# The prologue of a two-stage attention and feed-forward kernel, its TensorE steps in another order

## What is computed

```
q, k, v = relu(x @ Wqkv.T)                      per head of 8 channels
vk      = [v, 1].T @ k                          summed over the 512 tokens
num     = vk @ q ;  att = num[:8] / (num[8] + 1e-15)
x1      = layernorm(x + att @ Wproj.T + bias)
h       = silu(x1 @ Wg.T / 127) * (x1 @ Wu.T / 127)
out     = layernorm(x1 + h @ (Wd / 127).T)
```

## Time and profile before

| | |
|---|---|
| three runs | 490.69, 491.10, 489.64 us (median 490.69) |
| span of the profiled execution | 489.6 us |
| PE busy | 482.2 us, 98% |
| DVE, ACT, POOL busy | 415.5, 255.9, 85.2 us |
| granted TensorE clock, mean | 0.999 |
| first gate product of batch 0 starts | 40.2 us |

### The profile page before, as it was taken

One profiled execution on the slowest core, in us unless ns is written; L12 is line 12 of the kernel. 1 busy time (PEld: TensorE's weight loads), 2 busy tenths in 40 slices (PEclk: granted clock), 3 DMA queues, 4 the chain that ended last, 5 costly groups with the idle time before them and its releaser, 6 DMA issues.

```text
span 489.6 us, 11236 instructions
## 1 busy us (share of the span) xinstructions
PE 482.2 (98%) x4291; PEld 405.5 (83%) x4291; DVE 415.5 (85%) x939; ACT 255.9 (52%) x442; POOL 85.2 (17%) x94
## 2 busy tenths in 40 slices
PE   8999999999999999999999999999999999999996
PEld 5888888878888888888888888888888888879885
DVE  5878878879899797988979889797988979799896
ACT  4667435464455545545555455545555554355553
POOL 1330110402103030210402103030220402113012
PEclk9999999999999999999999999999999999999999
DMA  8425075274754737467283754737467281561212
GB/s 302 179 81 173 11 247 174 89 259 167 252 178 181 251 108 260 142 238 233 89 304 118 253 178 166 263 110 261 143 235 234 87 299 46 175 216 46 86 44 88
DMA packets 67656, 85.29 MB, mean 174 GB/s; under 512 B 4016, under 2 KB 47024, under 8 KB 67632
## 3 DMA queue, kind: packets, MB, share of 16 engines
q1 hardware_dynamic: 67344, 84.70, 50.2%
q10 hardware_dynamic: 288, 0.26, 0.2%
HBM read 48.24 MB, written 36.18 MB: 172 GB/s over the span
## 4 chain that ended last, share of the span: by engine, by line
PE 78%; DVE 11%; DMA 5%; issue 2%; ACT 2%; POOL 1%; SPq 0%; POOLq 0%; DVEq 0%
PE up_ps L1058 28%; PE abcd_ps L1058 22%; PE gate_ps L1058 22%; PE abcd_ps L1110 3%; DVE h L616 2%; PE gate_ps L1088 2%; DMA wd_raw<-x_way 2%; DVE st L685 2%; DVE h_lo L609 2%; DMA x_way<-wu_raw 1%; ACT h_hi L409 1%; DVE r L702 1%; DMA wkv_raw<-att_way 1%; DVE r L737 1%; DMA wqp_raw<-w_q 1%
## 5 line engine op out<-in xcount | busy, mean ns | idle before, releaser
L409 ACT ACTIVATE h_hi<-h 128x512 fp32r<-128x512 f32 (+1 forms) x97 | 60.6, 626 | 72.2 <-DVE h L616 71.7
L331 POOL TENSOR_TENSOR rstd<-ve,minus_half 128x4 f32<-128x4 f32 (+2 forms) x36 | 35.5, 985 | 339.8 <-DVE ve L697 338.6
L609 DVE TENSOR_TENSOR h_lo<-h,h_hi 128x512 fp32r<-128x512 f32 (+1 forms) x97 | 63.3, 678 | 25.6 <-ACT h_hi L409 25.3
L414 ACT ACTIVATE silu<-gate_ps 128x512 f32<-128x512 f32 x95 | 55.9, 588 | 45.6 <-PE gate_ps L1058 45.6
L616 DVE SCALAR_TENSOR_TENSOR h<-up_ps,silu 128x512 f32<-128x512 f32 x95 | 65.1, 686 | 16.6 <-PE up_ps L1058 13.9
L1058 PE MATMUL gate_ps<-x1T_hi,wg_hi 128*128 128x512 f32 x192 | 75.0, 391 | 1.3 <-ACT silu L414 0.7
L1058 PE MATMUL gate_ps<-x1T_lo,wg_hi 128*128 128x512 f32 x192 | 74.8, 390 | 0.0
L1058 PE MATMUL up_ps<-x1T_hi,wu_hi 128*128 128x512 f32 x192 | 74.8, 389 | 0.0
L1058 PE MATMUL up_ps<-x1T_lo,wu_hi 128*128 128x512 f32 x192 | 74.7, 389 | 0.0
L406 ACT ACTIVATE kv<-abcd_ps 128x512 f32<-128x512 f32 x55 | 32.9, 601 | 44.9 <-PE abcd_ps L1058 43.5
L354 POOL TENSOR_TENSOR xb<-x_raw,bias_sb 128x1024 f32<-128x1024 f32 x16 | 38.7, 2420 | 50.0 <-DVE den L639 47.8
(11 more groups left out here) (191 smaller groups left out, 1017.1 us busy)
## 6 DMA issues: line engine op xcount, KB each, us to landing
x_raw<-x_tok SPq DMA_DIRECT2D x16, 512.0 KB, 3.6
att_way<-wg_raw SPq DMA_DIRECT2D x30, 256.0 KB, 3.5
wkv_raw<-att_way SPq DMA_DIRECT2D x30, 256.0 KB, 3.0
xT_raw<-x_chan SPq DMA_DIRECT2D x14, 512.0 KB, 4.4
x_way<-wu_raw SPq DMA_DIRECT2D x28, 256.0 KB, 2.4
wd_raw<-x_way SPq DMA_DIRECT2D x28, 256.0 KB, 3.0
out<-out_sb SPq DMA_DIRECT2D x14, 512.0 KB, 3.4
x_keep<-r SPq DMA_DIRECT2D x12, 512.0 KB, 2.6
```

Of the source, the lines that this page charges most:

```text
L331: nc.gpsimd.tensor_tensor(rs[:, tiles], ve[:, tiles], minus_half[:, tiles], ALU.pow).then_inc(rs_ok, 1)
L409: nc.scalar.activation(dst, src, ACT.Copy).then_inc(ok, 1)
L414: nc.scalar.activation(silu[:, j % 2, :], gate_ps[bank_of(j)][:], ACT.Silu, scale=WSCALE).then_inc(silu_ok[j], 1)
L609: return nc.vector.tensor_tensor(lo, raw, f32(hi), ALU.subtract)
```

## The change

The order of the lists of TensorE, ScalarE and VectorE in the prologue is rewritten, and with it which banks some steps use:

- q of batch 1 moves from before vk of batch 0 to behind vk of batch 1. All four kv tiles of batch 1 now stand before the numerator of batch 0, and vk of batch 1 straight behind it. The banks of the kv tiles of batch 1 change places.
- One tile more of batch 2 stands before the projection of batch 0.
- The turn of x1 of batch 0 and the flag's product move from before the numerator of batch 1 to behind vk of batch 2; the flag's product uses a bank of its own (`flag_ps` in `up_ps1`).
- ScalarE takes relus and sums of squares in an order that fits. VectorE makes xT_lo of batch 2 before the denominator of batch 0, masks vk of batch 1 before attT_lo, and makes x1T_lo of batch 0 behind the denominator of batch 1.

```diff
-        kv1_ps = (gate_ps[0][:], up_ps[0][:], gate_ps[1][:], up_ps[1][:])
+        kv1_ps = (gate_ps[1][:], up_ps[1][:], gate_ps[0][:], up_ps[0][:])
+        flag_ps = up_ps[1][0:1, 0:3]
...
             xT_hi_of(2)
-            q_relu(1, (gate_ps[1][:], up_ps[1][:]))
...
-            kv_relu(0, 1, kv1_ps[0])
+            act.wait_ge(vk_mm, 1)
+            for t in range(NT):
+                kv_relu(t, 1, kv1_ps[t])
             squares_of(0, wg_lo)
-            for t in range(1, NT):
-                kv_relu(t, 1, kv1_ps[t])
+            squares_of(1, wu_lo)
+            q_relu(1, (gate_ps[1][:], up_ps[1][:]))
             attT_hi_of(0)
-            kv_relu(0, 2, kv2_ps[0])
-            squares_of(1, wu_lo)
+            for t in range(2):
+                kv_relu(t, 2, kv2_ps[t])
             squares_of(2, wd_lo)
-            for t in range(1, NT):
+            for t in range(2, NT):
                 kv_relu(t, 2, kv2_ps[t])
...
+            xT_lo_of(2)
             rden_of(0)
             att_of(0, turned=True)
-            xT_lo_of(2)
+            vk_of(1, vk1_ps)
             attT_lo_of(0)
-            vk_of(1, vk1_ps)
...
-            dve.wait_ge(flag_mm, 1)
-            nc.vector.reduce_sum(lo_flag[:], B[0:1, 0:3], AX.X).then_inc(flag_ok, 1)
-            x1T_lo_of(0)
...
             vk_of(2, vk2_ps)
+            dve.wait_ge(flag_mm, 1)
+            nc.vector.reduce_sum(lo_flag[:], flag_ps, AX.X).then_inc(flag_ok, 1)
             rden_of(1)
+            x1T_lo_of(0)
             att_of(1)
...
             pe.wait_ge(xT1_lo_ok, 1)
-            q_of(1, (gate_ps[1][:], up_ps[1][:]), xT1_hi, xT1_lo)
+            kv_of(0, 1, kv1_ps[0], xT1_hi, xT1_lo)
             pe.wait_ge(ones_ok, 1)
             vk_of(0, A)
-            kv_of(0, 1, kv1_ps[0], xT1_hi, xT1_lo)
+            for t in range(1, NT):
+                kv_of(t, 1, kv1_ps[t], xT1_hi, xT1_lo)
             num_inputs(0)
             num_of(0, qT_first)
-            kv_of(1, 1, kv1_ps[1], xT1_hi, xT1_lo)
-            for t in range(2, NT):
-                pe.wait_ge(q_ok[t - 2], 2)
-                kv_of(t, 1, kv1_ps[t], xT1_hi, xT1_lo)
+            vk_of(1, vk1_ps)
+            q_of(1, (gate_ps[1][:], up_ps[1][:]), xT1_hi, xT1_lo)
             pe.wait_ge(consts_in, 16)
             attT_of(0)
-            vk_of(1, vk1_ps)
             pe.wait_ge(xT_lo_ok, 2)
             kv_of(0, 2, kv2_ps[0])
+            pe.wait_ge(q_ok[0], 2)
+            kv_of(1, 2, kv2_ps[1])
             pe.wait_ge(wp_lo_ok, 1)
             proj_of(0)
-            for t in range(1, NT):
+            pe.wait_ge(q_ok[1], 2)
+            for t in range(2, NT):
                 kv_of(t, 2, kv2_ps[t])
-                if t == 2:
-                    pe.wait_ge(squares_ok, 3)
-                    mm(B[0:1, 0:3], ones_col[:], lo_squares[:], start=True, stop=True).then_inc(flag_mm, 1)
-            pe.wait_ge(vk_ok, 2)
-            pe.wait_ge(kv_ok[0], 3)
+            num_inputs(1)
+            for n in range(2):
+                pe.wait_ge(r1_ok[n], 1)
+            pe.wait_ge(kv_ok[NT - 1], 3)
+            num_of(1)
+            vk_of(2, vk2_ps)
+            pe.wait_ge(squares_ok, 3)
+            mm(flag_ps, ones_col[:], lo_squares[:], start=True, stop=True).then_inc(flag_mm, 1)
             x1T_pair(0, r2, x1T_ps, 1)
             x1T_pair(1, r2, x1T_ps, 1)
             pe.wait_ge(flag_ok, 1)
             pe.reg_load(flag, lo_flag[:].bitcast(INT32))
-            pe.wait_ge(kv_ok[NT - 1], 3)
-            num_inputs(1)
-            num_of(1)
-            vk_of(2, vk2_ps)
             q_of(2, q2_ps, ahead_of_second=lambda: pe.wait_ge(vk_ok, 3))
```

## The result

The changed kernel takes **491.84 us** (median of 12 runs, 490.97 to 492.76), the kernel before, in the same comparison, 490.87 us (12 runs, 489.64 to 491.83). The ratio is 1.0019 (95% interval 1.001 to 1.0028), so the change costs about 0.97 us, between 0.5 and 1.4. That is within 0.3%: no difference by the measure that the prediction used, on its slower side.

The account below looks back on a forecast made before the run. TensorE, busy 482.2 of 489.6 us, was taken to bound the kernel. Waits of 0.39, 0.89 and 0.20 us less 0.6 of passages made 0.86, added to the 490.69 median: 491.55 us, range 490.2 to 492.6.

Parts of the forecast that it names:

- Wait 1: Before the turn of batch 0's attention, TensorE stands 0.39 us until VectorE has made att; bounds 0.2 and 0.6.
- Wait 2: Before the numerator of batch 1, TensorE waits 0.89 us for ScalarE's relu to empty bank A; between 0.8 and 1.0.
- Wait 3: Before q of batch 2, TensorE waits 0.20 us for the flag's sum and register load; bounds 0 and 0.55.
- The passages: In the prologue, fewer changes from narrow to wide products on TensorE save about 0.6 us, at about 0.23 us each.
- the third block: Numerator of batch 1, vk of batch 2, flag, then x1's turn and q: passage between 0 and 0.23 us, taken as 0.11.
- The waits are covered: Rival for the prologue: passages save 0.7 us and only half of wait 2 remains, giving 490.4 us; chance 0.09.
- the change doesn't do what it says: Rival: the new order is not really built; given nothing, as the built order shows every step moved.
- The stall near 99 us goes: Rival in batch 2's turn: TensorE's 0.7 us wait for x1T_lo vanishes, giving 490.85 us; chance 0.13.
- The trip of batch 1's att: Slower rival: its second half lands late and the projection waits some 0.75 us, giving 492.3 us; chance 0.08.
- The load was not long: Judges the slower rival at the flag: a register load of 1.3 us gives 492.35 us; chance 0.04.
- VectorE's x1T_lo for gate: Ahead of the first gate product: ready for both halves near 40.2, 0.8 us ahead of gate.

Follow-up runs that it names:

- cover_num: Changed kernel with the first half of q of batch 2 and the flag's product put before the numerator of batch 1: 491.67 us, ratio to before 1.0015.
- load_later: Changed kernel with the flag's register load moved behind q of batch 2: 491.53 us, ratio to before 1.001.
- cover_both: As cover_num, with one tile of batch 2 moved ahead of the turn of batch 0's attention and a third ahead of the projection: 491.31 us, ratio 1.0002.
- tail_only: Kernel before with only the new order from the numerator of batch 1 on, the head as before: 491.74 us, ratio to before 1.001.
- cover_both_again: The cover_both kernel, unchanged, for a second execution under the profile: 491.03 us, ratio to before 1.0000.
- head_only: Changed kernel with the tail of before, flag's product and both turns of x1 ahead of the numerator of batch 1: 491.91 us, ratio to before 1.0024.

## Why the prediction was right

**The forecast.** 491.55 us was foretold and 491.84 measured, with the difference from before +0.86 against +0.97 (and 0.6 the second time). The first gate product was to stand at 41.08 and stands at 40.96. The places foretold on the way held to a tenth: vk of batch 0 at 14.97 (14.97), the numerator at 19.95 (20.01), the turn at 25.03 (25.01), the numerator of batch 1 at 35.20 (35.22), the transposes at 37.18 (37.09). That a sum is right does not show that its terms are; they are taken one by one.

**Wait 1** was put at 0.39 us. q's last product starts at 24.48 (the second of the row at 24.25), the next could start at 24.70, and the turn starts at 25.01: 0.31. The chain from the numerator over den, rden and att to the turn runs as copied from the earlier trace rows. VectorE's rows of after show that step by step:

```profile
21.31 0.29 DVE L641 TENSOR_SCALAR den<-abcd_ps 128x128 f32<-128x128 f32 x1 [0.65 <-PE abcd_ps L1112]
21.64 0.95 DVE L645 RECIPROCAL rden<-den 128x128 f32<-128x128 f32 x1
```

Such a wait need not be in the list of waits: here only the chain and the timeline show it.

**Wait 2** was put at 0.89 us. The last product starts at 34.06, the numerator could follow at 34.38 and starts at 35.22: 0.84, of which the trace marks 0.78 as waiting for kv. It was the dearest term, and it was the bank conflict in the code. cover_num keeps that conflict and puts work over it, and gives 0.60 us of the stretch back net.

**Wait 3** was put at 0.20 us. Against the transposes' own step it looks like 0.11 (their last start is 37.91, the next could be at 38.02, q starts at 38.13). But load_later, where q does not wait, takes it up 0.13 behind the last pair, and the changed kernel 0.33: the wait is 0.20, and its price in the stretch 0.17. What was off is the flag's product. I gave it 0.12 us of its own behind vk, as it takes in the chain of before (at 32.95). In the trace it starts at 36.94, ahead of the last product of vk, and the transposes follow at 37.09 and not at 37.18:

```profile
36.38 0.75 PE L1090 MATMUL gate_ps<-kv 128*32 128x36 f32 x63
36.94 0.17 PE L1323 MATMUL up_ps<-lo_squares,ones_col 128*1 128x3 f32 x1
36.95 0.20 PE L1090 MATMUL gate_ps<-kv 128*32 128x36 f32 x1
```

This did not bring VectorE's sum forward, which starts at 37.42 (37.39 foretold):

```profile
37.42 0.14 DVE L927 TENSOR_REDUCE lo_flag<-up_ps 1x1 f32<-1x3 f32 x1
```

But the load stood closer behind the sum than the 0.29 us that I had read from the earlier trace rows, whose start of the load is rounded to a tenth. It began at 37.6 and not at 37.68, and q 0.12 us before its time. The load's own time was right:

```profile
L1327 PEldq TENSOR_LOAD <-lo_flag x1: 484/484/484, 37.6 to 37.6; - x1
```

The rule of the Trainium skill that was weighed (DMA: Bandwidth & Descriptors, Latency and other measured facts: a floor of about 600 ns for a tensor_load) is not borne out: the load took 0.484 to 0.488 us in the traces shown here.

**The passages** were to save 0.6 us. The waits measured are 0.31 + 0.84 + 0.20 = 1.35, the loss is 0.74, so 0.61 were saved. What was too high is waits 1 and 2, by 0.08 and 0.05, and that makes up the difference of the forecast's 0.86 from 0.74. That the saving came out so close is luck in part: the third block costs 0.17 on the way into the transposes and 0.03 on the way out, 0.20 where I took 0.11, and the flag's product costs nothing where I kept 0.12. The two errors cancel. What cover_both wins is smaller, 0.33, which the count bears out roughly: it has three full passages left of five (vk of batch 0, vk of batch 1, vk of batch 2), 2 x 0.23 saved, less 0.15 for the transposes behind the numerator and 0.03 for the products behind the turn of att, 0.28. That narrow work bundled is a gain was right. What it needs is cover for every wait that the bundle opens.

That it is the *width* of the products that makes a passage dear is not shown. In the rows the narrow products also use a smaller block of weights (128*32 and 64*64 against 128*128 for wide products and transposes). The transposes are narrow and use the whole block, and leaving them costs 0.03; this speaks for the block, or for widths below 128. No run changes one without the other.

**The rivals.** "The waits are covered" and "the change doesn't do what it says" did not happen. "The stall near 99 us goes" did happen in the profiled execution (none where the earlier trace rows had 0.7) but as something that varies, so it did not move the median by 0.7. The trip of batch 1's att does not meet ScalarE: its relay is read back at 48.62, and the projection follows the second block at 51.84 with no wait.

```profile
48.62 1.14 ACT L410 ACTIVATE attT_hi<-wkv_raw 128x512 fp32r<-128x512 f32 x2
```

The load was not long. VectorE's x1T_lo for gate ended at 39.92, a microsecond ahead. The shares of the forecast do not quite follow from its terms: the upper bounds of the three waits add up to 492.2 and not to 492.1, and 492.1 lay within what could not be told apart, not beyond it.

**One step was wrong and cost nothing.** I set the span against the median and took 1.1 us to lie between them. The run that is profiled has its own time: 490.97 for the span 488.9, 491.84 for tail_only's 489.8, 490.17 for cover_num's 488.1, 489.43 for cover_both_again's 487.4. It is 2.0 to 2.1 us each time. So the profiled execution of before, 489.6, was one of about 491.7 us, at the upper end of its runs, and both of its later waits were long. The forecast came out close because the difference was added to the median. Had it been added to the profiled time, it would have been 492.5.

**What stays open.** In cover_both (twice), tail_only and head_only a batch of the loop takes 29.47 us and not 29.44. The 0.03 us times the ten or so batches are about 0.3 us, as much as cover_both wins in the prologue, and would account for a time that is that of before. It recurs in both executions of cover_both, so it seems to belong to the kernel. In one batch of the loop followed step by step it lies behind vk: the first half of q takes 1.49 us by its starts in cover_both (210.88 to 212.37) and 1.46 before (210.90 to 212.36). The loop's code is the same, and what makes it is not found. Nor do stretch and loop give every median: cover_num's lies 0.6 us above what they say, and tail_only's 0.4 us below, the latter within its interval. None of the versions beats the kernel before by more than can be measured.

## What to carry to other kernels

When narrow and wide products alternate on TensorE, bundling the narrow ones saves a tenth or two of a microsecond for each passage saved. Before bundling, list for each of them which bank it overwrites and who must empty it, and leave as much other work between as that takes (here 1.16 us from the start of the last product through the relu to the start of the next). Where a row names an engine as the cause of a wait, follow the chain back; here a transfer stood behind silu. Test the halves of a reordering singly and together: here each half's price depended on the other, and the first half alone was the dearest. Compare stretches of a trace for effects below 1 us, not spans.

## What the runs showed of the hardware

- Two waits of a trace come and go between executions of the same kernel: 0.84 us and none near 434 us in cover_both, 0.66 and 0.40 near 99 us before. The one near 434 us goes with the time of one transfer out of DRAM, 4.25 to 4.70 us in six executions and 3.02 to 3.08 in four. Together with the moment at which the stretch starts (13.3 to 13.9 us) they can account for 2 us, about the scatter between the runs of one kernel. TensorE's stretch in the prologue repeats to 0.02 us.
- The flag's product (two rows of one column of weights) takes 0.12 us in the chain between wide products (before) and slips in among the narrow products of vk without a time of its own (after: vk starts at 36.38 and the transposes 0.71 us later, where vk alone takes 0.70).
- A passage from the products of 36 and 72 columns to those of 512 costs 0.23 us. Into the 128-column transposes it costs 0.15 to 0.17 (0.37 and 0.39 for a pair in place of 0.22), and from them to 512 columns 0.03 (1.39 in place of 1.36).
- A register load on TensorE took 0.484 to 0.488 us in each trace shown, and it runs ahead of products listed before it: in the changed kernel it starts at 37.6 while transposes start until 37.91. 0.17 us of the stretch came back by setting it behind the next products.
